# Attention and expert layers on 8 cores: the output normalisation of each half moved behind its last W2 phase

## What is computed

```python
x = x + ln(attn(ln(x)))            # 16 heads, causal, ALiBi bias
def ffn(x):                        # x is ln of the line above
    z = ln(x) * g + b
    w = top-2 softmax weights of z @ rW over 8 experts
    hid = gelu(z @ W1[e] + b1[e])  # every expert, every token, hidden 2048
    return x + sum_e w[e] * (hid @ W2[e] + b2[e])
x = x + ln(ffn(ln(x)))
```

## Time and profile before

| | us |
|---|---|
| median of the runs shown (2 runs) | 3366.36 |
| lowest and highest of them | 3200.7 and 3532.01 |
| the profiled execution | 3203.41 |
| span of its slowest core (core 1) | 3201.9 |
| TensorE matmul busy | 2783.3 (87%) |
| VectorE busy | 954.4 (30%) |
| ScalarE busy | 986.4 (31%) |

### The profile page before, as it was taken

The page is one execution under the profiler, slowest core; times in us unless marked ns, Lnnn a source line. Parts: engine busy times, 40 slices in busy tenths (PEclk is TensorE's granted clock), DMA queues, the critical chain, the costliest instruction groups (busy, mean ns, idle before and its releaser), DMA issues.

```text
span 3201.9 us, 40073 instructions; the slowest of 8 cores (3182.1 to 3201.9 us)
## 1 busy us (share of the span) xinstructions
PE 2783.3 (87%) x11536; PEld 1409.3 (44%) x18304; DVE 954.4 (30%) x1670; ACT 986.4 (31%) x1989; POOL 64.7 (2%) x78
## 2 busy tenths in 40 slices
PE   1768889988888855699999999998599999999996
PEld 1435554222222222345555555554255555555553
DVE  4455333556555467310110011004120011011005
ACT  0001656666666568402112211221202211211221
POOL 0000000000000000000000000000000000000000
PEclk9988555555555577799999999999799999999998
DMA  5121000000000254536435543644716434642542
GB/s 132 27 40 27 1 1 1 1 1 1 1 1 1 46 143 153 121 52 105 63 62 87 87 69 55 106 79 106 149 35 106 79 59 74 106 70 52 90 79 92
DMA packets 92893, 205.06 MB, mean 64 GB/s; under 512 B 4248, under 2 KB 12568, under 8 KB 92704
## 3 DMA queue, kind: packets, MB, share of 16 engines
q0 software_dynamic: 75952, 142.64, 27.6%
q1 hardware_dynamic: 16752, 59.85, 5.9%
HBM read 319.96 MB, written 25.17 MB: 108 GB/s over the span
## 4 chain that ended last, share of the span: by engine, by line
PE 79%; DMA 9%; DVE 5%; ACT 2%; issue 2%; DVEq 2%; ACTq 0%; SPq 0%
PE pb L962 28%; PE pb L996 25%; PE pb L483 11%; PE pb L449 9%; PE pb L328 4%; DMA x0t<-x 3%; PE pb L376 2%; DVE recf_s L511 2%; DMA xuscr<-x1t 2%; DMA y<-outb 1%; DMA xuscr<-ut 1%; DMA x1r<-xuscr 1%; ACT slabs L457 1%; PE pb L533 1%; DVE outb L924 1%
## 5 line engine op out<-in xcount | busy, mean ns | idle before, releaser
L962 PE MATMUL pb<-Trz,fsl 128*128 128x512 bf16 x4096 | 905.0, 384 | 3.8 <-DVE accB L1010 3.8
L996 PE MATMUL pb<-fsl,hidT 128*128 128x512 bf16 x4096 | 893.8, 381 | 11.0 <-DVE accB L1010 7.9
L970 ACT ACTIVATE hidT<-pb,b_s 128x512 bf16<-128x512 f32 x512 | 324.5, 685 | 1385.6 <-PE pb L962 1383.1
L457 ACT ACTIVATE slabs<-pb,alibi_s 128x512 bf16<-128x512 f32 (+2 forms) x896 | 451.1, 554 | 504.9 <-PE pb L449 504.9
L962 PEld LDWEIGHTS pb<-Trz,fsl 128*128 128x128 bf16 x4096 | 397.0, 97 | 165.3 <-issue 8.2
L996 PEld LDWEIGHTS pb<-fsl,hidT 128*128 128x128 bf16 x4096 | 396.4, 97 | 162.8 <-issue 3.3
L483 PE MATMUL pb<-slabs,vgD 128*65 128x512 bf16 (+2 forms) x836 | 348.5, 512 | 54.1 <-DVE slabs L465 54.0
L1007 DVE SCALAR_TENSOR_TENSOR accA<-pb,wS,accA 128x512 f32<-128x512 f32 x64 | 48.1, 751 | 1097.7 <-PE pb L996 1097.3
L449 PE MATMUL pb<-qT,kT 64*128 64x512 bf16 (+2 forms) x896 | 320.1, 472 | 50.6 <-ACT slabs L457 38.8
L955 PEld LDWEIGHTS <-fsl 128*128 128x128 bf16 x2048 | 202.4, 99 | 257.2 <-issue 22.3
L989 PEld LDWEIGHTS <-hidT 128*128 128x128 bf16 x2048 | 201.2, 98 | 257.3 <-issue 18.2
(11 more groups left out here) (109 smaller groups left out, 1165.0 us busy)
## 6 DMA issues: line engine op xcount, KB each, us to landing
fsl<-W POOLq DMA_DIRECT2D x64, 2048.0 KB, 15.7
xpp<-x SPq DMA_DIRECT2D x8, 1024.0 KB, 4.9
x0t<-x SPq DMA_DIRECT2D x16, 512.0 KB, 4.3
xuscr<-x1t SPq DMA_DIRECT2D x16, 512.0 KB, 3.2
xuscr<-ut SPq DMA_DIRECT2D x16, 512.0 KB, 3.1
x1r<-xuscr SPq DMA_DIRECT2D x8, 1024.0 KB, 6.8
y<-outb SPq DMA_DIRECT2D x8, 1024.0 KB, 4.0
accA<-xuscr SPq DMA_DIRECT2D x8, 512.0 KB, 4.5
```

The source lines that it names most:

```text
L457: e.activation(slab, sb[:, 0:qw], AF.Exp, bias=bias, scale=0.125),
L962: tw=tw: e.matmul(b[:, 0:tw], lw, rhs, start=(cc == 0), stop=(cc == CCH - 1)),
L970: e.activation(dst, b[:, 0:tw], AF.Gelu, bias=b1_s[:, e_ * FCH + fc: e_ * FCH + fc + 1], scale=1.0),
L996: e.matmul(b[:, 0:512], lw, rhs, start=(fc == 0), stop=(fc == FCH - 1)),
```

## The change

The finals are no longer emitted pair by pair inside the W2 phase of expert 7. All eight of a half are emitted in one loop behind that phase, and behind the emission of the two weight loads that follow it. The statistics of a final get a wait for the accumulation of their own tile.

```diff
         acc_reload_sd = {}
+        final_stt = {}
         acc_b2d = {}
@@ emit_final
-            d_fs = S.add("vector", fstat, inc=sDVE)
+            d_fs = S.add("vector", fstat,
+                         waits=[(sDVE, final_stt.get((th, i), 0))], inc=sDVE)
@@ the loop over halves and experts
                     rd[w2_bids[0]] = (sDVE, d_st)
                     rd[w2_bids[1]] = (sDVE, d_st)
-                    if e_ == E - 1 and t8 % 2 == 1:
-                        emit_final(th, t8 - 1)
-                        emit_final(th, t8)
+                    if e_ == E - 1:
+                        final_stt[(th, t8)] = d_st
                 ffn_w_load(nth, ne, 1, 1)
                 ffn_w_load(nth, ne, 2, 0)
+                if e_ == E - 1:
+                    for i in range(THC):
+                        emit_final(th, i)
```

## The result

| | before | after |
|---|---|---|
| median of all executions, us | 3209.54 (10) | 3275.04 (11) |
| profiled execution, us | 3203.41 | 3272.54 |
| spans of the cores in it, us | 3182.1 to 3201.9 | 3253.9 to 3271.0 |
| ratio to before, 95% interval | | 1.0197 (1.0171 to 1.0224) |

The changed kernel is about 2.0% slower, with an interval that lies on both sides of the 2% line. The profiled execution is 69.1 us longer. The direction and the order of the waits were forecast; the size, +78.6 us, was too large, and most of what the moved work itself fell short of it lies at the end of half 0.

A forecast was written before the change was run, and what follows sets the result against it. TensorE, busy 87% of the span, was taken as the bound. Core 1: +41.4 - 5.2 at half 0, +41.4 at the end, 3281.0 us; core 2: +81.8, 3284.1 us. Forecast 3282 us, +2.5%, range 3265 to 3295 us.

The forecast's parts named there:

- The order of the queues: End of half 0: VectorE, SyncE and ScalarE queues carry the finals' delay into TensorE; its stand grows from 21.73 to 77 us.
- the added wait: On VectorE, each final's statistics wait for its own earlier accumulate; taken as costing nothing, at most 0.1 us for each of 16.
- One sign: End of the kernel: the last store should be issued 41 us later after the last matmul than before.
- The later start: Both halves: finals start six token tiles later, behind the accumulate of tile 7 instead of tile 1, 41.4 us.
- The length of the chain in half 0: First statistics to the output of tile 6: kept at 72.9 us, one pair again slowed by weight loads.
- The recorded sign of being wrong: Prediction would be wrong if the chain of finals shortened once the accumulates are out of it.
- What comes back: End of half 0: earlier accA reload shrinks TensorE's second stand to 1.68 us; 5.2 us back on core 1, 1.0 on core 2.
- The choice of the core: Slowest core decides: core 1 gives 3281.0 us, core 2 3284.1 us; 3282 us taken, between the two.
- Finals hidden: Rival: half 1's W1 runs over half 0's finals, 33.5 us saved, 41.4 us lost at the end; 3211 us, chance 0.07.
- No slowing by weight loads: Rival, half 0: pair 1's transfers find DMA engines free, chain 56.75 instead of 72.9 us; 3265 to 3268 us, chance 0.14.
- Two pairs slowed: Rival, half 0: the second weight load also slows the next pair's store and load, another 12 us; 3294 us, chance 0.07.
- TensorE's clock: After the long stand: return priced at nothing new; rival of lower clock throughout seven stretches, 38 us, 3320 us, chance 0.05.

The follow-up runs named there:

- k1: Changed kernel with only half 0's finals behind its W2 phase, half 1 keeping the order of before; 1.0072 of the time before.
- k2: Changed kernel with only half 1's finals behind its W2 phase, half 0 keeping the order of before; 1.0127 of the time before.
- k6: Changed kernel with half 1's accumulator set-up moved to W1 chunks 8 to 15, roots staying on ScalarE; 1.0218 of the time before.
- k4: Changed kernel with the finals' reciprocal roots worked out on VectorE instead of ScalarE; 1.0300 of the time before, 3302.9 us.
- k3: Changed kernel with half 0's two weight loads emitted behind the finals, waiting for the last one; 1.0177 of the time before.
- k5: Changed kernel with roots on VectorE and half 1's accumulator set-up moved to W1 chunks 8 to 15; 1.0253 of the time before.
- v1: Kernel before with two pairs of x1r buffers and half 1's accumulator set-up in W1 chunks 8 to 15; 0.9866 of the time before.
- v4: v1 with the finals of a pair taken together: both statistics, both roots, both outputs; 0.9817 of the time before, 3144.9 us.

## Why the prediction was right or wrong

**The order of the queues.** Right: W2 in one piece of 55 us, accumulations 6.9 us apart, stand at the first b2 product (77 us forecast, 75.14 us on core 7, 70.6 us as a mean), second stand 1.68 us, the added wait at no cost. One sign was worded wrongly: the last store comes 50 us later after the last matmul than before (68.2 us on core 7, 18.0 us on core 1 before), since W2 itself ends earlier; from the start of W2 it is 43.2 us on these two cores.

**The later start.** Right: 41.44 us at both halves, and each half pays alone (k1, k2). B grew by 40.3 us for 41.4 us; its chain was 0.7 us shorter.

**The length of the chain in half 0.** This is the term that failed: it was put at no change, and it shrank by 3.3 us as a mean. I kept the 72.9 us of core 1, saying that "one pair is slowed, the first instead of the third". That is what happened, but the length was 66.6 us. Two things are in it. Core 1 had one of the longest chains of before; the mean over the cores was 70.0 us. And the step beside the weight loads took 21.8 us after and 24.0 us before as a mean. The likely reason is the first load's 13 us to itself: the two loads were 15.2 us apart after and 22.9 us before. I had the remark that the free start spoke for the rival, and gave its effect nothing. The other 1.1 us lie in the two steps that no weight load touches, 12.8 and 13.2 us before, 12.4 and 12.5 us after. The recorded sign of being wrong, a chain that shortens once the accumulations are out of it, is thus met in half 0 by this much at most; half 1 doesn't confirm it (k1, k2), and the cause stays open.

**What comes back.** The second term that was mis-sized, a gain taken too small. The path from the output of tile 6 to TensorE's resumption took 9.15 us before and after, as forecast. From there to the next W2 phase it was 79.6 us before and 74.4 us after as a mean, 5.2 us back, 3.9 us of them in the second stand (5.6 us before, 1.68 us after). On core 1 I had taken 5.2 us, but on core 2 only 1.0 us. Together the half cost 41.4 - 3.3 - 5.2 = 32.9 us, where the prediction had 36.2 us (core 1) to 40.4 us (core 2).

**The choice of the core.** I added the growth of core 2, +81.8 us, to a core that was near the slowest already, in one execution. Which core is the slowest changes from run to run, with some 6 us of difference in the work ahead of the change (first row of the table above); and the profiled execution of before, 3203.4 us, was itself at the lower end of its kind, 3200.7 to 3226.2 us. The measured ratio times 3203.4 us is 3266.5 us. So the change cost 73 us by the stretches, 67 us by the mean spans (which hold the 5.6 us of the first row) and 63 us by the ratio, where I had 78.6 us. The forecast lay 14.5 us above the 2% line, and these misses together used it up; 0.86 for a clear loss was too sure.

**The rivals.** "Finals hidden" fell: GELU stays behind the last root (k6), and with the root gone the reload takes its place (k4). "No slowing by weight loads" fell too: the step beside them is 21.8 us and falls to 12.8 us without them (k3). "Two pairs slowed" didn't happen: the steps after the first were 12.4 and 12.5 us. TensorE's clock: the first 32 matmuls after the stand took 9.18 us as a mean over the cores before (stands of 18 to 23 us, single cores 8.5 to 9.7 us) and 9.25 us after (stands of 68 to 75 us, 8.8 to 9.9 us); the long stand costs nothing more, and the later stretches of the changed kernel stay under 9 us, as forecast. On core 7 the granted clock was 0.50, the 1.2 GHz level, from 2226 to 2300 us, through most of the stand and the first 4.3 us behind it, and 0.93 in the 5 us after. The Trainium skill ("TensorE: Matmul & The Clock Gate", section "HAM oscillation — how this bites in real kernels") says that TensorE starts cold, at the lower clock, after such a gap; these rows agree.

## What to carry to other kernels

Work moved later in one engine's program delays everything that other engines' programs have placed behind it, even where the moved work is off the bound engine; look at what stands right behind it on each queue. A wait taken off TensorE is worth nothing if a second stand follows a few matmuls later, and freeing one wall only shows the next if both wait for the same chain. Shorten the chain instead: a second pair of buffers, here taken from tiles that had served their turn, brought the changed kernel from 1.020 to 1.007 of the time before and the kernel before to 0.988. Work that is let through earlier can also set free transfers that slow the chain (k5).

## What the runs showed that was not expected

The same reciprocal root takes VectorE about 4 us as 14 operations on 128 x 1 elements, 0.15 to 0.27 us each with 0.08 us between them, and ScalarE 1.2 us in four (core 7 of the changed kernel, 2222.54 to 2223.74): moving it made each half 14 us longer. And in v1 and v4 stretches of 16 matmuls between waits of only 1.7 us alternate between 3.63 and 5.31 us, as the stretches of 32 mostly did in the kernel before (7.08 and about 8.75 us). The granted clock shows it on core 7 of the changed kernel: 1.00 in the wait of 1.68 us at 2305.4, 0.50 in the matmuls from 2307.7 to 2310, 0.92 in the 6 us after. Short waits of TensorE at a set-up cost its clock too, though not at every one.
